# Attention with a second, transposed set of scores instead of transposed exponentials, and written out without loops

## What is computed

```python
# L1
attn = jnp.einsum('bhnd,bhdm->bhnm', q, k) * scale
attn = jax.nn.softmax(attn, axis=-1)
out = jnp.einsum('bhnm,bhmd->bhnd', attn, v)
...
# L3
sw_mask = (j <= i) & (j > i - WIN)
logits = jnp.where(sw_mask[None, None], logits, jnp.float32(-jnp.inf))
attn = jax.nn.softmax(logits, axis=-1)
...
# the whole
x = _L0_conv_ref(x, ...)
x = x + _L1_conv_ref(_gn(x), ...)
t = _to_tokens(x)
t = t + _L2_attn_ref(_ln_t(t))
t = t + _L2_ffn_ref(_ln_t(t), ...)
t = t + _L3_attn_ref(_ln_t(t), ...)
t = t + _L3_ffn_ref(_ln_t(t), ...)
```

## Time and profile before

| | before |
|---|---|
| median of 3 runs | 834.06 us (831.86 to 834.90) |
| the profiled execution | 833.0 us, span 831.3 us |
| PE busy | 596.5 us (72%), mean granted clock 0.86 |
| DVE busy | 523.9 us (63%) |
| ACT busy | 408.8 us (49%) |
| POOL busy | 267.2 us (32%) |
| q1 transfers | 34.23 MB, 14.7% of 16 engines |

### The profile page before, as it was taken

How to read it: one execution, slowest core, us unless ns; L and a number is a source line. 1 busy time by engine, 2 the same in 40 slices (tenths; PEclk the granted TensorE clock), 3 DMA queues, 4 the chain that set the end, 5 groups by cost and what they waited for, 6 DMA issues and landing times. The chain is left out here.

```text
span 831.3 us, 12531 instructions
## 1 busy us (share of the span) xinstructions
PE 596.5 (72%) x2930; PEld 344.3 (41%) x2930; DVE 523.9 (63%) x1165; ACT 408.8 (49%) x989; POOL 267.2 (32%) x496
## 2 busy tenths in 40 slices
PE   4764358787546589999999999941414888746998
PEld 4652136565335464444344344320203666534332
DVE  2784468887428637769869868727275777604443
ACT  2432458787424257665665665621315777613222
POOL 3110002333310017766766766705050233320000
PEclk9995779999868679999999999965556999956999
DMA  1072562321000000000000000000504433000000
GB/s 43 27 223 78 157 163 62 92 64 37 2 32 19 1 0 1 1 1 0 0 0 0 0 0 0 0 26 6 147 12 128 105 87 101 1 0 0 13 13 25
DMA packets 32664, 34.63 MB, mean 42 GB/s; under 512 B 8042, under 2 KB 25460, under 8 KB 32628
## 3 DMA queue, kind: packets, MB, share of 16 engines
q1 hardware_dynamic: 32628, 34.23, 14.7%
HBM read 23.72 MB, written 7.34 MB: 37 GB/s over the span
## 5 line engine op out<-in xcount | busy, mean ns | idle before, releaser
L1345 POOL TENSOR_TENSOR vall<-g_s 128x512 f32<-128x512 f32 x128 | 162.4, 1272 | 95.7 <-ACT g_s L1329 91.5
L1304 DVE TENSOR_TENSOR z_s<-bank,PB 128x1024 f32<-128x1024 f32 x128 | 155.6, 1223 | 56.1 <-PE bank L1271 48.5
L1329 ACT ACTIVATE g_s<-z_s,b 128x1024 f32<-128x1024 f32 x128 | 146.9, 1148 | 84.1 <-DVE z_s L1304 82.0
L1278 PE MATMUL bank<-vall,W 128*128 128x512 f32 x256 | 131.7, 598 | 6.5 <-ACT y_s L1324 4.1
L1271 PE MATMUL bank<-XN_C,W 128*128 (+1 forms) x256 | 130.2, 592 | 1.0 <-PEq L1201 1.0
L908 ACT ACTIVATE E_s<-bank,negmax 128x256 f32<-128x256 f32 (+2 forms) x256 | 107.6, 435 | 44.2 <-DVE negmax L941 43.3
L949 DVE COPY ET_s<-bank 128x512 f32<-128x512 f32 (+1 forms) x112 | 69.4, 619 | 30.9 <-PE bank L794 16.0
L941 DVE TENSOR_REDUCE negmax<-bank 128x2 f32<-128x512 f32 (+1 forms) x128 | 72.4, 576 | 16.1 <-PE bank L780 7.5
L1278 PEld LDWEIGHTS bank<-vall,W 128*128 128x128 f32 x256 | 47.1, 190 | 72.9 <-issue 49.3
L1271 PEld LDWEIGHTS bank<-XN_C,W 128*128 128x128 f32 x256 | 48.1, 190 | 59.1 <-issue 57.0
L799 PE MATMUL bank<-ident,E_s 128*128 128x128 f32 x256 | 41.7, 289 | 17.3 <-ACT E_s L908 10.9
(11 more groups left out here) (241 smaller groups left out, 1029.5 us busy)
## 6 DMA issues: line engine op xcount, KB each, us to landing
stack<-qk_parts SPq DMA_DIRECT2D x128, 64.0 KB, 2.2
qk_parts<-parts SPq DMA_DIRECT2D x48, 128.0 KB, 2.0
stack<-qk_parts SPq DMA_DIRECT2D x32, 192.0 KB, 3.1
W<-in_L_ffn_W_dram SPq DMA_DIRECT2D x1, 2048.0 KB, 8.8
xs<-XN_C SPq DMA_DIRECT2D x8, 256.0 KB, 2.4
stack<-qk_parts SPq DMA_DIRECT2D x16, 128.0 KB, 3.3
xs<-in_x_dram SPq DMA_DIRECT2D x8, 128.0 KB, 2.0
xs<-XN_C SPq DMA_DIRECT2D x8, 128.0 KB, 2.0
```

What stands on the lines that cost most here:

```text
L1278: nc.tensor.matmul(bank[7][:, :], W2[:, f % FT, :], h_s[:, f % RING, :], start=(f % FT == 0), stop=(f % FT == FT - 1)).then_inc(s_D.sem, 1)
L1304: nc.vector.tensor_tensor(z_s[:, s % RING, :].rearrange("p (w n) -> p w n", w=2), bank[s % 4][:, None, :].broadcast_to([P, 2, W]), PB[:, b ...
L1329: nc.scalar.activation(g_s[:, s % RING_G, :], z_s[:, s % RING, :], ACT.Gelu, bias=b1[:, s:s + 1]).then_inc(s_g.sem, 1)
L1345: nc.gpsimd.tensor_tensor(h_s[:, s % RING, :], g_s[:, s % RING_G, 0:W], g_s[:, s % RING_G, W:2 * W], ALU.add).then_inc(s_h.sem, 1)
```

## The change

`attention` is rewritten for both stages. The first set of scores (two banks now) only feeds DVE's maxima. POOL splits the negated maxima of four heads into three bf16 parts (`parts_of_shifts`), PE turns them onto rows (`turn_shifts`) and ACT stores them as `shift_rows`. PE then makes the scores a second time with keys on partitions (`scoresT`, three banks): a selector product with `pick` adds the shift of each query, in L3 after the band `bandTb`. ACT's exponential of that has no bias and no accumulator and is already in the form that the product with V takes. V has a column of ones for each head (`ROWS` = 17, in `vall` itself), so the sums come out of the same product. PE turns the output (four transposes), DVE inverts the sums and scales, PE turns it back, ACT stores, PE projects with a 128x128 `Wp`. The residual is added in place in `R`, the normalised form goes straight into `XN_T`; `v_pad`, `rx`, `keep` are gone, and no chain raises `idle`.

All steps are written out: there is no loop in `attention`. The stack comes by half images, six transfers each; both halves of images 0 and 1 are read in the preparation, the later ones when the transposed scores of the half four before are done. In the prologue POOL builds `bandTb` and `pick`; `Wp_raw` and the padded `Wo3` are gone (one transfer for eight). Of the diff, cut to its core:

```diff
-        STACK_DMAS = len(BLOCKS_Q) + 3
+        STACK_DMAS = 6
...
                     if i == 1:
                         sp.wait_ge(s_out[0].sem, s_out[0].after(0))
-                        read_stack(sp, bass.ds(0, 1), 0, qk_in[0])
+                        for image in range(PAIR):
+                            for half in range(2):
+                                read_stack(sp, image, half, qk_in[image][half])
...
+        RING_T = 3
+        AT_T, AT_ROWS, AT_PV = 7, 6, 11
+        AT_OT, AT_ON, AT_Y, AT_XN, AT_XT = 17, 19, 20, 25, 30
...
+                    for g in range(2 * PAIR, HALVES):
+                        sp.wait_ge(s_T, (g - 2 * PAIR + 1) * SLOTS)
+                        read_stack(sp, g // 2, g % 2, qk_in[g // 2 % PAIR][g % 2])
...
+                    def turn_shifts(g):
+                        pe.wait_ge(s_sp, g + 1)
...
+                            for t in range(NT):
+                                ins = nc.tensor.matmul(bank[6][:, t * P:(t + 1) * P], of[:, t, :, :].rearrange("p j r -> p (j r)"),
+                                                       identb[:, :], start=True, stop=True)
...
+                    def scoresT(u):
...
+                        if j == 0:
+                            pe.wait_ge(s_rows, g + 1)
+                        if u >= RING_T:
+                            pe.wait_ge(s_E, u - RING_T + 1)
...
+                            nc.tensor.matmul(to[:, :].rearrange("p (t n) -> p t n", t=NT), pick[:, j, :],
+                                             shift_rows[:, g % 2, None, 0:N].broadcast_to([P, NT, N]),
+                                             start=True, stop=False, skip_group_check=True)
+                            nc.tensor.matmul(to[:, 0:N], k[:, 0:P], q, start=False, stop=False, skip_group_check=True)
+                            nc.tensor.matmul(to[:, N:2 * N], k[:, P:N], q,
+                                             start=False, stop=True, skip_group_check=True).then_inc(s_T, 1)
...
+                    for s in range(LAST):
+                        if s == 0:
+                            scores(s)
+                        if s + 1 < UNITS:
+                            scores(s + 1)
+                        if (g := half_at(s, AT_ROWS)) is not None:
+                            turn_shifts(g)
+                        if 0 <= s - AT_T < UNITS:
+                            scoresT(s - AT_T)
+                        if (g := half_at(s, AT_PV)) is not None:
+                            values(g)
...
+                            nc.scalar.activation(ET_all[:, u % TURNED, 0:width], bank[2 + u % RING_T][:, 0:width],
+                                                 ACT.Exp).then_inc(s_E, 1)
...
-                    link = Chain(pool, s_link_p, idle)
+                    link = Chain(pool, s_link_p)
...
+                    def parts_of_shifts(g):
+                        pool.wait_ge(s_nm, (g + 1) * SLOTS)
+                        if g >= 2:
+                            pool.wait_ge(s_sr, g - 1)
+                        m = negmax[:, g // 2 % PAIR, g % 2 * SLOTS:(g % 2 + 1) * SLOTS, :].rearrange("p h t -> p t h")
+                        to, rest = shifts[:, g % 2, :, :, :], rest_m[:, g % 2, :, :]
+                        link(nc.gpsimd.tensor_copy(to[:, :, :, 0], m))
+                        link(nc.gpsimd.tensor_tensor(rest, m, to[:, :, :, 0], ALU.subtract))
+                        link(nc.gpsimd.tensor_copy(to[:, :, :, 1], rest))
+                        nc.gpsimd.tensor_tensor(to[:, :, :, 2], rest, to[:, :, :, 1], ALU.subtract).then_inc(s_sp, 1)
...
+                    for s in range(LAST):
+                        if (g := half_at(s, SLOTS)) is not None:
+                            parts_of_shifts(g)
+                        if (n := image_at(s, AT_Y + 1)) is not None:
+                            rsqrt_image(n)
```

More of the change, by code:

```diff
@@ L38 @@
 TURNED = 2 * SLOTS
+ROWS = HD + 1
 EXPERTS = 8
@@ L602, in write_parts, with read_stack @@
                              parts[:, b, part, kind, :].rearrange("p (b n) -> p b n", n=N)).then_inc(done.sem, 16)
[L604 to L612, removed]
+        def read_stack(sp, image, half, done):
+            b = image % PAIR
+            heads = slice(half * SLOTS, (half + 1) * SLOTS)
+            rows = [qk_dram[image, kind, :, :, :].rearrange("a (d h) n -> (a d) h n", h=HEADS)[:, heads, :] for kind in range(2)]
+            for kind, blocks in ((0, ((0, 3, 0), (3, 3, 1), (6, 2, 2))), (1, ((0, 3, None), (3, 3, None), (6, 2, None)))):
+                for n, count, part in blocks:
+                    to = stack[n * HD:(n + count) * HD, b, half, kind, :, :]
+                    if part is None:
+                        sp.dma_start(to, rows[kind][0:count * HD, :, :]).then_inc(done, 16)
+                    else:
+                        of = rows[kind][part * HD:(part + 1) * HD, :, :]
+                        sp.dma_start(to, of[None, :, :, :].broadcast_to([count, HD, SLOTS, N])).then_inc(done, 16)
         xs_in = [signal(f"l1_xs_in{b}", 16) for b in range(2)]
@@ L619, in bass_conv_attn_hybrid_kernel @@
         s_out = [signal(f"l1_parts_in_dram{b}", 6 * 16, True) for b in range(2)]
-        s_vpad = sem("v_pads_set")
-        qk_in = [signal(f"l1_stack_in{b}", STACK_DMAS * 16) for b in range(PAIR)]
+        s_vpad = sem("l1_pads_set")
+        qk_in = [[sem(f"l1_stack_in{b}{half}") for half in range(2)] for b in range(PAIR)]
         with nc.Block() as block:
@@ L877, in _ @@
+                        if (n := image_at(s, AT_XT)) is not None:
+                            pe.wait_ge(s_xn, n + 1)
+                            pe.wait_ge(s_r, min(n + 2, IMAGES))
+                            for t in range(NT):
+                                ins = nc.tensor.transpose(bank[7][:, t * P:(t + 1) * P],
+                                                          XN_T[:, n * N + t * P:n * N + (t + 1) * P], ident[:, :])
+                            ins.then_inc(s_xT, 1)
                 @block.scalar
@@ L1389, in _ @@
                         sp.wait_ge(s_out[0].sem, s_out[0].after(0))
-                        read_stack(sp, bass.ds(0, 1), 0, qk_in3[0])
+                        for image in range(PAIR):
+                            for half in range(2):
+                                read_stack(sp, image, half, qk_in3[image][half])
                     for b in range(2):
```

499 lines of the change are left out of this document (208 added, 291 removed).

## The result

The changed kernel takes 864.5 us in the median (858.8 to 869.3, four runs) beside 834.5 for the kernel before on the same chips: ratio 1.038, interval 1.033 to 1.043. It is slower by 30 us where 815 us, 19 less, were forecast. The profiled execution has a span of 867.0 us against 831.3.

A forecast was written before the change was run, and what follows sets the result against it. DVE was taken to set L1's beat. From 833.0 us, gains of 16.3 (L1) and 7.7 (L3) and costs of 3.7 (prologue) and 1.5 (L1 preparation) gave 814.2, forecast as 815 with the median's 1.1 offset; range 803 to 835.

The forecast's parts named there:

- What bounded the kernel before: L1 attention: DVE sets the beat, its work per image summing to 12.3 us against a shortest interval of 12.34.
- The change per image: Attention stages: DVE falls from 12.3 to 6.8 us in L1; PE's own sum becomes 9.0 (L1) and about 8.7 (L3).
- the listing: One interval between images worked out, engine by engine, before clock loss: 11.3 us in L1, 10.4 in L3.
- The clock's share: Attention intervals: 0.7 us added in L1 and 0.5 in L3 for TensorE's clock, giving 12.0 and 10.9.
- The stack's supply: Attention stages: keys and queries land about 4.8 us after the request, against 5.05 of lead, so no stall.
- the signs named for being wrong: PE waiting for POOL's split or DMA in each image, L1's head over 21 us, or tail growth over 3.
- supply late: Rival, 14%: keys and queries land 5.8 to 6.0 us after request; PE waits 0.7 (L1), 1.2 (L3), five times each: 825.
- the loop through POOL: Rival, 13%: root, split, transposed scores and projection form a closed path of 14.35 and 13.4 us: 848; threshold 26.7 for both intervals.
- The estimate from the Trainium skill: Stack supply in attention: 2.3 + 0.4 + about 2 us fixed transfer cost = 4.7 us, no stall.
- Costs elsewhere: Prologue loses 3.7 us on POOL, L1 preparation 1.5 (0 to 4) through late writes, L3 preparation nothing.
- Jumps: Attention loops: by instruction fetch alone, removing 3 jumps in two stages saves some 2.6 us; twice the code costs nothing.
- POOL does not quicken: Rival, 9%: POOL's chained steps stay at 0.375 us, intervals 12.85 (L1) and 12.0 (L3), tails 4.0 longer: 834, no change.

The follow-up runs named there:

- the kernel with five buffers: Changed kernel with five half-image buffers for keys and queries instead of four, in both attention stages: 822.5 us, ratio 0.986 to the kernel before.

## Why the prediction was wrong

*What bounded the kernel before: right in the main, with luck in the sum.* A shorter root on POOL left L1's beat at 13.68, and DVE is the busiest engine in it. But 12.3 met the shortest interval of 12.34 by luck: it adds durations of 0.68 us of instructions that start 0.60 apart. DVE's busy time there is 11.11; the rest are short waits.

*The change per image: right.* With the stack in time the beat is 11.38 and 10.45 where the listing had 11.3 and 10.4, and PE waits where it said, for the maxima behind an addition. An exponential of 512 took 0.60 (0.61 forecast), a split 1.11 (1.05), a chained step 0.28 (0.26), the wait for a maximum up to 1.2 (1.5). One thing was not listed: in L3 PE also waits for POOL's split, 4.5 us in six places. The stages of the kernel with five buffers are 17.4 and 8.6 us shorter than before; 16.3 and 7.7 were forecast.

*The clock's share: wrong, small.* I added 0.7 and 0.5 us for cold work. With five buffers, and so no long stand inside an interval, none was lost: the granted clock is 1.00 in an interval of either stage (169.42 to 180.81 and 674.0 to 684.5). That is 3.2 and 2.2 us over five intervals (56.8 and 52.3 for 60.0 and 54.5). About three were lost again in heads (22.6 and 19.8 for 21.2 and 19.1) and tails (26.7 and 26.0, cut as the prediction cut them, for 26.3 and 25.3).

*The stack's supply: the step that failed.* "I take no stall" rested on 4.8 us from request to use against a lead of 5.05. The lead was 4.7 to 5.05 at eight of the 13 stands and 5.0 in the mean, near enough. The term that failed is the 4.8, and PE waiting for DMA in each image was one of the signs named for being wrong. Six issues of 0.45 end at 2.7 (2.3 is where the last one starts), which leaves 2.1 behind them. Issuing was 3.5, since the reads with a repeated source take 0.70 and not 0.45 to issue. And the row's 3.1 behind the last issue for a whole image was scaled down for half the bytes, though the change also altered the shape of the transfers: no source repeated there. It was 3.8 in the mean. Together 7.4, a stall of 2.5. The rival "supply late" had the mechanism and put it at 0.7 and 1.2 us a stall, 10 us in all; it was 2.5 on average in 13 stalls, 42 us by the medians with the clock (864.5 against 822.5 with a fifth buffer). The rival nearest in time, the loop through POOL with 848, was not at work: PE waited for POOL's split for 0.9 us in L1 and 3.2 in L3. The estimate from the Trainium skill in the prediction, 4.7, failed with mine. The section that it took the 2 us from describes transfers that GpSimd issues, and these are SP's. The 2 us fit the kernel before, where SP's reads of 16 rows landed 2.1 us after their issue began; but the estimate knows completion and bytes, but not how few engines carried them. A sentence of the same page on that was not weighed.

*Costs elsewhere.* The prologue lost 3.9 (3.7 forecast). L1's preparation lost 7.0, and not 1.5: I had 0.45 for each of 24 reads, and they took 0.61, 14.65 us against 10.8; so the writes started 8.0 late and not 4.2; and issued back to back they took 8.1 us where I had 5.4 to 7.0, so 1.0 was given back and not 2.7. L3's preparation lost nothing, as said. Jumps: without loops the intervals from the second to the fifth are alike to 0.01 us. That is in line with rows 6, but the loops went together with much else, and no run shows their price alone.

*"POOL does not quicken" at 834* was undersized: 860 with everything else in time. The listing's 12.85 for L1 let PE stand once behind POOL; measured is 14.1, near the 14.35 of the other rival, and 13.4 in L3, as that rival had it. By this the two were one rival, and its threshold was near.

*What stays open.* L0 and FFN vary by up to 3 and 4 us between profiled executions of kernels that have them alike; nothing here says why. Which DMA engines carried the reads with a repeated source, and why one such request took 6.8 us and another 8.0, is open too.

## What to carry to other kernels

Before a change shortens a beat, work out for every ring of buffers how long a refill takes from its request, issues and bytes apart, and compare it with the new beat times the steps of lead; a refill of fewer transfers was not quicker here, where their outer dimension was 2 or 3. A ring that was late by 2.5 us about once per image cost 42 us, and one more half buffer, 4 KB a partition, gave them back. And count a chained step on a slow engine as part of a closed path: 0.1 us in each was worth 38 us.

## What the runs showed of the hardware

Issuing a read took SP 0.70 us where the source repeats a block and 0.45 where it doesn't, whether it moved 2 or 4 heads. Behind 1 MB just issued, three more repeated reads of whole images took 6.0 us to issue where the first three took 2.4. Reads whose source repeats 2 or 3 blocks ran out in a tail at about 70 GB/s; as blocks of 16 rows they didn't. A semaphore increment between two chained POOL steps costs 0.11 us (0.28 to 0.39). V products of the same shape take 1.06 us at the upper and 1.91 at the lower clock.
